# A fused convolution and state-space kernel on one core: the layer norm spread over three tiles, with a PSUM bank of its own

## What is computed

```
layer 0: two 3x3 convolutions with binary weights, batch norms, out = relu(y*scale + shift + x)
layer 1: mu, var over the 64 channels of each pixel
         xn = (x - mu) / sqrt(var + eps) * ln_g + ln_b
         the channels are cut into 4 chunks of 16; each is a sequence of 3136 steps
         y = chunk + mamba(chunk):
             xi, z = in_proj(chunk);  u = silu(conv4(xi));  dt, B, C = x_proj(u)
             delta = softplus(dt_proj(dt));  h = h*exp(delta*A) + delta*u*B;  y = h.C + u*D
             out_proj(y * silu(z))
layer 2: 1x1, grouped 3x3, 1x1 convolution, residual
layer 3: four directional scans with relu(conv)
```

## Time and profile before

| what | value |
|---|---|
| median of 3 runs | 9415.61 us (9406.84 to 9419.84) |
| the profiled execution's own time | 9422.56 us |
| its span, first to last instruction | 9419.6 us |
| mean granted clock of TensorE | 0.869 of full speed |
| busy in the span | PE 82%, DVE 70%, ACT 57%, POOL 54% |
| layer 1's loop, 16 pairs of 14 tiles | about 725 to 7070 us |

### The profile page before, as it was taken

The page is one execution under the profiler, slowest core; times in us unless marked ns, Lnnn a source line. Parts: engine busy times, 40 slices in busy tenths (PEclk is TensorE's granted clock), DMA queues, the critical chain, the costliest instruction groups (busy, mean ns, idle before and its releaser), DMA issues.

```text
span 9419.6 us, 132034 instructions
## 1 busy us (share of the span) xinstructions
PE 7733.7 (82%) x30601; PEld 4129.2 (44%) x30601; DVE 6595.7 (70%) x9126; ACT 5400.0 (57%) x9444; POOL 5115.0 (54%) x3388
## 2 busy tenths in 40 slices
PE   9977777777777777777787777777778999999996
PEld 9962222222222222222222222222224899959996
DVE  7748898898988989889898998989882122211222
ACT  0237777777777777777777777777770133201332
POOL 0007788887877878788787887878770000000000
PEclk9988788888878888788888888888888999999998
DMA  9646565665656556565565665655551000030002
GB/s 177 167 115 172 154 171 158 168 165 156 171 158 166 163 157 168 156 167 161 163 168 156 167 164 160 170 158 168 160 164 58 18 0 0 18 86 0 0 0 55
DMA packets 1108311, 1201.77 MB, mean 128 GB/s; under 512 B 460432, under 2 KB 1094800, under 8 KB 1107344
## 3 DMA queue, kind: packets, MB, share of 16 engines
q1 hardware_dynamic: 871568, 1117.24, 43.7%
q10 hardware_dynamic: 236032, 77.08, 3.5%
HBM read 961.04 MB, written 155.41 MB: 119 GB/s over the span
## 4 chain that ended last, share of the span: by engine, by line
PE 38%; issue 22%; DVE 16%; POOL 9%; ACT 8%; DVEq 1%; ACTq 1%; DMA 0%; POOLq 0%; SPq 0%
PE ps L921 18%; DVE ps L631 11%; PE ps L908 5%; DVE da L647 5%; POOL prod L658 4%; PE ps L226 3%; PE ps L417 3%; PE ps L669 3%; ACT da L621 2%; POOL dlt L551 2%; PE ps L431 2%; ACT L1020 1%; ACT L1018 1%; POOL lnx L503 1%; PE ps L666 1%
## 5 line engine op out<-in xcount | busy, mean ns | idle before, releaser
L658 POOL TENSOR_TENSOR prod<-da,bsp 128x896 f32<-128x896 f32 x1792 | 3439.5, 1927 | 1040.9 <-PE ps L669 702.7
L647 DVE TENSOR_TENSOR_SCAN da<-da,ps 128x449 f32<-128x449 f32 (+1 forms) x3584 | 3863.2, 1078 | 0.0
L631 DVE TENSOR_TENSOR ps<-ps,bsp 128x448 f32<-128x448 f32 x3585 | 2198.4, 613 | 767.7 <-PE ps L615 741.6
L621 ACT ACTIVATE da<-da,nega 128x448 f32<-128x448 f32 x3588 | 2257.6, 662 | 56.6 <-issue 48.1
L615 PE MATMUL ps<-stack,seld 96*128 96x448 bf16 x3587 | 1440.2, 416 | 810.3 <-DVE da L647 765.0
L921 PE MATMUL ps<-pv,ws 128*128 128x224 f32 x8800 | 1695.2, 355 | 9.4 <-ACT pv L1083 7.1
L921 PEld LDWEIGHTS ps<-pv,ws 128*128 128x128 f32 x8800 | 1660.2, 189 | 45.0 <-issue 7.7
L669 PE MATMUL ps<-prod,wc 128*32 128x448 f32 x7200 | 1405.8, 686 | 191.7 <-POOL prod L658 191.1
L615 PEld LDWEIGHTS ps<-stack,seld 96*128 96x128 bf16 x3587 | 356.1, 101 | 2335.9 <-DVE da L647 2016.8
L1247 DVE SCALAR_TENSOR_TENSOR pv<-ps,R 128x224 f32<-128x224 f32 x880 | 422.3, 480 | 1282.1 <-PE ps L921 1282.1
L417 PE MATMUL ps<-xn,wtap 128*128 128x448 f32 x1808 | 1017.3, 671 | 3.5 <-ACT bsp L477 3.5
(11 more groups left out here) (119 smaller groups left out, 7227.7 us busy)
## 6 DMA issues: line engine op xcount, KB each, us to landing
da<-delta_copy SPq DMA_DIRECT2D x3595, 224.0 KB, 3.5
stack<-parts SPq DMA_DIRECT2D x2700, 28.0 KB, 2.3
delta_copy<-dlt SPq DMA_DIRECT2D x225, 224.0 KB, 2.9
lnx<-in_x SPq DMA_DIRECT2D x118, 224.0 KB, 3.0
lny<-y_nchw SPq DMA_DIRECT2D x118, 224.0 KB, 4.1
x_column_pairs<-otile SPq DMA_DIRECT2D x225, 116.0 KB, 3.3
xpad<-x_column_pairs SPq DMA_DIRECT2D x32, 812.0 KB, 4.4
xpad<-in_x SPq DMA_DIRECT2D x64, 392.0 KB, 6.6
```

What stands on the lines that cost most here:

```text
L621: a.activation(elements(j, st.t), elements(j, st.t), ACT.Exp, scale=nega[:, j:j + 1])\
L631: v.tensor_tensor(du, du, bsp[:, st.t % 2, 0, :], ALU.mult).then_inc(S["dbu_done"], 1)
L647: v.tensor_tensor_scan(a, a, d, start, ALU.mult, ALU.add).then_inc(S["scan_done"], 1)
L658: g.tensor_tensor(prod[:, j % 8:j % 8 + 2, :], da[:, j:j + 2, lo:lo + T], bsp[:, st.t % 2, 1:2, :].to_broadcast([P, 2, T]), ALU.mult).then ...
```

## The change

The layer norm of a block no longer runs inside one tile. Its first part (`ln_in`: the loads, `scale_y`, `add_x`) runs in tiles 6 to 12, its middle (`ln_mid`: `relu`, `lnc`, `lnv`) one tile later, in tiles 7 to 13, its end (`ln_last`: `times_rstd`, `shift`) one tile later again, in tiles 8 to 13 and tile 0 of the next pair. The loads move from ahead of SP's slot 0 to slot 6. The number of instructions of each kind in the loop stays as it was.

The two matmuls write to bank 4, which only they use, and have semaphores of their own: `lnc` waits until ACT has read the previous `lnv` and for its input, `lnv` waits for ACT's square. They leave the list of tasks that take turns in banks 5 and 6, so all 14 tiles have the five tasks `u`, `z`, `bc0`, `dt`, `bc1` there. Ahead of the loop seven blocks are begun instead of six; the seventh does not do its end there.

```
-PE_AT = {0: ["tap0"], 1: ["last3", "tap1"], 2: ["tap2", "tap3"], 3: ["z"], 4: ["project"], 5: ["lnc"], 6: ["bc0"],
-         7: ["dt"], 8: ["sum0", "bc1"], 9: ["lnv"], 11: ["sum1"], 14: ["sum2"]}
-ACT_AT = {0: ["scale_y"], 2: ["cast0"], 3: ["relu"], 4: ["cast1"], 5: ["silu", "u", "z", "exp"], 6: ["evacuate"],
-          7: ["lnc"], 8: ["bc0"], 9: ["dt"], 10: ["dt2", "bc1"], 11: ["lnv"], 13: ["clamp"], 15: ["shift"]}
+PE_AT = {0: ["tap0"], 1: ["last3", "tap1"], 2: ["tap2", "tap3"], 3: ["z"], 4: ["project"], 6: ["bc0"], 7: ["dt"],
+         8: ["sum0", "bc1"], 10: ["lnc"], 11: ["sum1"], 13: ["lnv"], 14: ["sum2"]}
+ACT_AT = {2: ["cast0"], 3: ["relu"], 4: ["cast1"], 5: ["silu", "u", "z", "exp"], 6: ["evacuate"], 7: ["shift"],
+          8: ["bc0"], 9: ["dt"], 10: ["dt2", "bc1"], 11: ["scale_y"], 12: ["lnc"], 13: ["clamp"], 15: ["lnv"]}
-POOL_AT = {1: ["rest0", "add_x"], 5: ["rest1"], 9: ["over"], 11: ["delta"], 13: ["delta_u", "times_rstd"]}
-SP_AT = {1: ["copy"], 5: ["part0"], 7: ["part1"], 9: ["part2"], 12: ["store"]}
+POOL_AT = {1: ["rest0"], 3: ["times_rstd"], 5: ["rest1"], 9: ["over"], 11: ["delta"], 13: ["delta_u"], 15: ["add_x"]}
+SP_AT = {1: ["copy"], 5: ["part0"], 6: ["ln_load"], 7: ["part1"], 9: ["part2"], 12: ["store"]}
...
-        DU_BANK, TMP_BANK, Y_BANK, O_BANK = 0, 5, 7, 7
+        DU_BANK, LN_BANK, TMP_BANK, Y_BANK, O_BANK = 0, 4, 5, 7, 7
...
+                self.ln_in = Norm(p, t, 6) if 6 <= t <= 12 else None
+                self.ln_mid = Norm(p, t, 7) if t < 0 or 7 <= t <= 13 else None
+                self.ln_last = Norm(p, t, 8) if t == 0 or t >= 8 else None
...
+        def ln_centre(pe, st):
+            n = st.ln_mid.ln
+            if not (st.ahead and st.k == 0):
+                pe.wait_ge(S["var_copied"], n)
+            pe.wait_ge(S["x_relu"], n + 1)
+            pe.matmul(ps[:, LN_BANK, 0:T], wcs("centre", 0, P), xres[:, :], start=True, stop=True)\
+                .then_inc(S["centre_mm"], 1)
+
+        def ln_average(pe, st):
+            n = st.ln_mid.ln
+            pe.wait_ge(S["squared"], n + 1)
+            pe.matmul(ps[:, LN_BANK, 0:T], wcs("average", 0, P), xsq[:, :], start=True, stop=True)\
+                .then_inc(S["average_mm"], 1)
...
-            for k in range(6):
+            for k in range(7):
                 st = Ahead(k)
-                pe_task(pe, st, "lnc")
-                pe_task(pe, st, "lnv")
+                ln_centre(pe, st)
+                ln_average(pe, st)
```

More of the change, by code:

```diff
@@ L316, in build @@
         BC = ["bc0", "bc1"]
-        AHEAD = [(n, k) for k in range(6) for n in ("lnc", "lnv")] + [(n, 0) for n in ["u", "z", "dt"] + BC] + \
-            [(n, 1) for n in ("u", "z", "dt")]
+        AHEAD = [(n, 0) for n in ["u", "z", "dt"] + BC] + [(n, 1) for n in ("u", "z", "dt")]
         BASE = len(AHEAD)
@@ L323, in build @@
             for name in TASKS:
[L324 to L325 removed]
+                AT[(t, name)] = len(AT)
         ORDER = list(AT)
@@ L341, in drives, with __init__ @@
             return ps[:, DU_BANK + bank, lo:hi]
+        class Norm:
+            def __init__(self, p, t, first):
+                self.ahead = False
+                self.k = t - first if t >= first else t - first + ST
+                self.ln = p * KT + (self.k + (KT if t >= first else 0))
+                self.pair = (p + 1) % PAIRS
+                self.out = p * ST + t
+        class First:
+            def __init__(self, k):
+                self.ahead, self.k, self.ln, self.pair, self.out = True, k, k, 0, 0
         class Step:
@@ L370, in two_back @@
                 st = Step(self.p, t if i >= 0 else t - ST)
-                return back, st.next if back.startswith("bc") else st.ln if back.startswith("ln") else st.far
+                return back, st.next if back.startswith("bc") else st.far
         class Ahead:
@@ L478, in act_task @@
             elif name == "lnc":
-                if not (st.ahead and st.k == 0):
-                    a.wait_ge(S["xn_ready"], st.ln)
+                ln = st.ln_mid
+                if not (ln.ahead and ln.k == 0):
+                    a.wait_ge(S["xn_ready"], ln.ln)
                 a.copy(xcen[:, :], src).then_inc(S["centred"], 1)
@@ L483, in act_task, with ln_load @@
             else:
+                ln = st.ln_mid
                 a.activation(xvar[:, :], src, ACT.Ln, bias=vec_c(5)).then_inc(S["var_copied"], 1)
-                a.wait_ge(S["var_copied"], st.ln + 1)
+                a.wait_ge(S["var_copied"], ln.ln + 1)
                 a.activation(xrstd[:, :], xvar[:, :], ACT.Exp, scale=-0.5).then_inc(S["rstd"], 1)
[L489 to L492, removed]
+        def ln_load(sp, ln):
+            if not (ln.ahead and ln.k == 0):
+                sp.wait_ge(S["x_relu"], ln.ln)
+            a = ln.k * T
@@ L503, in ln_sum, with ln_relu, ln_scale @@
             g.tensor_tensor(lnx[:, :], lnx[:, :], lny[:, :], ALU.add).then_inc(S["x_summed"], 1)
[L505 to L508, removed]
+        def ln_relu(a, ln):
+            a.wait_ge(S["x_summed"], ln.ln + 1)
+            if not (ln.ahead and ln.k == 0):
+                a.wait_ge(S["centred"], ln.ln)
             a.activation(xres[:, :], lnx[:, :], ACT.Relu).then_inc(S["x_relu"], 1)
-        def ln_scale(g, st):
-            g.wait_ge(S["rstd"], st.ln + 1)
+        def ln_scale(g, ln):
+            g.wait_ge(S["rstd"], ln.ln + 1)
@@ L513, in ln_scale, with ln_shift @@
             g.tensor_tensor(xcen[:, :], xcen[:, :], xrstd[:, :], ALU.mult).then_inc(S["scaled"], 1)
[L515 to L519, removed]
+        def ln_shift(a, ln):
+            a.wait_ge(S["scaled"], ln.ln + 1)
+            if not ln.ahead:
+                a.wait_ge(S["out_mm"], ln.out + 2)
+            k = ln.k * T + 3
             a.activation(xn[:, k:k + T], xcen[:, :], ACT.Identity, bias=vec_c(1), scale=vec_c(0)).then_inc(S["xn_ready"], 1)
@@ L868, in _ @@
                                 conv_tap(pe, st, int(name[3:]))
-                            elif st.has_ln or not name.startswith("ln"):
+                            elif name == "lnc":
+                                if st.ln_mid:
+                                    ln_centre(pe, st)
+                            elif name == "lnv":
+                                if st.ln_mid:
+                                    ln_average(pe, st)
+                            else:
                                 pe_task(pe, st, name)
@@ L985, in _ @@
             a.wait_ge(S["ready"], 4)
[L986 to L992, removed]
+            for k in range(7):
+                ln = First(k)
+                ln_affine(a, ln)
+                ln_relu(a, ln)
+                act_task(a, Ahead(k), "lnc")
+                act_task(a, Ahead(k), "lnv")
+                if k < 6:
+                    ln_shift(a, ln)
             for k in range(2):
@@ L1264, in _ @@
             g.wait_ge(S["ready"], 4)
[L1265 to L1268, removed]
+            for k in range(7):
+                ln = First(k)
+                ln_sum(g, ln)
+                if k < 6:
+                    ln_scale(g, ln)
             st = Ahead(0)
@@ L1292, in _ @@
                                 rest_of(g, st, int(name[4]))
[L1293 to L1297, removed]
+                            elif name == "add_x":
+                                if st.ln_in:
+                                    ln_sum(g, st.ln_in)
+                            elif st.ln_last:
+                                ln_scale(g, st.ln_last)
             barrier(g, 3)
```

59 lines of the change are left out of this document (24 added, 35 removed).

## The result

The changed kernel takes 9091.33 us (median of 4 runs, 9089.95 to 9092.64), the kernel before beside it 9412.89 us (4 runs). The ratio is 0.9658, 95% interval 0.9641 to 0.9675. Forecast were 9105 us, in a range of 8960 to 9290. The profiled execution took 9091.03 us.

What follows compares the result with a forecast made beforehand. A ring through ACT and POOL, as long as the quiet tile, was taken to bound it beside DVE. Terms summed to 376.4 us a pair, 20.1 less; 16 x 20.1 - 10.6 = 311 us off gave 9112, so 9105, range 8960 to 9290.

Steps and rivals of the forecast that it cites:

- Waits removed: Bank waits of `lnc` and `dt`, `shift`'s and `relu`'s waits go; each tile starts at 25.34 us, 354.8 a pair.
- `add_x` in POOL's leg: At POOL's slot 15, between `over` and `rest0`, tiles 6 to 12: paid in full, 7.8 us a pair.
- `shift` in ACT's leg: At ACT's slot 7, tiles 8 to 13 and 0: costs 4.6 us a pair.
- `scale_y` and `lnc` ahead of `clamp`: On ACT, slots 11 and 12: POOL's `delta` waits for `clamp`, 1.04 us in tiles 7 to 12; sum 6.8.
- Free pieces: `relu` and `lnv` on ACT ahead of `cast1`, `times_rstd` on POOL between `rest0` and `over`: covered by idle time, no cost.
- The jump back: At the loop's top, ACT's jump before `cast0`: free by 1 us or up to 3.45; 1.0 a pair taken.
- PE's wait ahead of `lnv`: At PE's slot 13, waiting 2.2 us for ACT's squares; cost put at zero, between 0 and 3.8.
- Waits not shown by the rows: Other waits in ACT's leg of layer-norm tiles: 0.2 us a tile, 1.4 a pair, bounds 0 and 10.4.
- Ahead of the loop: One more block in series before the loop, hidden by nothing: 10.6 us.
- The rival in which DVE alone holds the tiles: DVE's work sets the tile time and the layer norm becomes free: 8759 us, or 8884 with `add_x` paid; 11%.
- The rival of a loss by `lnv`'s wait: PE's lead gives no cover, DVE stands 3.8 us in each of seven tiles: 9530 us; 5%.
- No change: The stalls only move and each tile with layer norm costs what it did; 4%.

Runs made afterwards that it cites:

- the spare POOL instruction at slot 3: The changed kernel with one more POOL addition of 128x448 on scratch tiles at slot 3 of tiles 1 to 5: 9090.07 us.
- The kernel with `lnv` later: The changed kernel with PE's `lnv` moved from slot 13 to slot 14, behind `sum2`: 9101.19 us.
- the spare instruction at slot 15: The changed kernel with one more POOL addition of 128x448 on scratch tiles at slot 15 of tiles 1 to 5: 9156.24 us.
- the last experiment: Against the one with both legs clear, ACT's instruction adding one to `dexp` left out of every tile, so the softplus is incomplete: 8664.71 us.
- the one with both legs clear: The changed kernel with `scale_y`, `lnc`, `shift` behind `clamp`, `lnv` at PE's slot 14, `add_x` at POOL's slot 3, loads a tile earlier: 8788.04 us.

## Why the prediction was right, step by step

The mechanism was right, and so were nearly all terms of the sum: a pair was put at 376.4 us and takes 375.3. That is 17 us of the 21 by which the profiled execution lies below the 9112 forecast for it.

1. *Waits removed.* The bank waits and `shift`'s wait went, and the quiet tiles stayed at 25.25 us. That `relu`'s wait on `add_x` would go was wrong. I took POOL's slot 15 of one tile to be earlier than ACT's slot 3 of the next, by the numbers of the slots. ACT runs ahead of POOL, and waits 1.76 us. It cost nothing, since it is spent ahead of `cast1`, where ACT waits for `rest0` in any case. In all, this wait is 198.4 us where it was 220.7.
2. *`add_x` in POOL's leg*: 7.8 us a pair put down. Taken out it gave 116 us (8904.45 to 8788.04), 7.3 a pair.
3. *`shift` in ACT's leg*: 4.6 put down; ACT's leg has 0.65 more, and taking it out gave 66 us, 4.1 a pair.
4. *`scale_y` and `lnc` ahead of `clamp`*: 6.8 put down. POOL waited 1.06 to 1.22 us a tile instead of 1.04, 123.1 us in all, 7.7 a pair; moving them behind `clamp` gave 121 us, 7.5 a pair. This is the term that was put too low. The slack of 0.48 us was read in one tile, and the wait is 1.06 us in one tile and 1.22 in the next.
5. *Free pieces*: the spare POOL instruction at slot 3 shows that this place costs nothing, and so did `times_rstd` and `add_x` together there. `relu` and `lnv` on ACT were free as well: in the tile shown ACT still waits 1.89 us for `rest0` behind them.
6. *The jump back*: 1.0 us a pair put down. ACT still stands at the loop's top, now 2.59 us, but POOL comes to `rest0` without a gap in the timeline of tile 0. Before, it had waited there 50.4 us in 15 pairs, for `cast0`; the trace after has no such wait, so none of it was paid:

```profile
2614.44 1.79 ACT L640 ACTIVATE da<-da,nega 128x448 f32<-128x448 f32 x3 [2.59 <-issue]
...
2615.11 3.66 POOL L677 TENSOR_TENSOR prod<-da,bsp 128x896 f32<-128x896 f32 x2
...
2618.73 1.03 POOL L587 TENSOR_TENSOR rest<-dlt,parts 128x448 f32<-128x448 f32 x1
```

7. *PE's wait ahead of `lnv`*: 2.2 us predicted, 2.52 measured. I had DVE covered by PE's lead; it is not quite, DVE waits 0.69 us behind it in the tile shown. That is free for another reason than the one I gave: DVE has 170.00 - 151.67 = 18.3 us of waits in these six tiles whatever their places. The kernel with `lnv` later has the wait removed and gains nothing.
8. *Waits not shown by the rows*: 1.4 put down, nothing found in the tile shown: `over` starts at 2868.67, 0.07 us after `dq` ends. Over a pair, the terms as the trace after has them are 354.8 + 7 x 1.13 for `add_x` + 7 x 0.65 for `shift` + 7.7 for `clamp` = 375.0, against 375.3 measured. That leaves 0.3 for this item and the jump together, of 2.4 put down. The 2.1 too much stood against the 0.9 that item 4 was too low, and that the sum came out within 1.1 is in part luck.
9. *Ahead of the loop*: 10.6 put down, 10.7 measured.

The rival in which DVE alone holds the tiles fell for this change, by the spare instruction at slot 15 and by the ring's waits in every tile. Only in the last experiment is DVE full too, at 99.3%. The Trainium skill (Perfetto Trace Analysis, "Identifying the Most-Contended Engine") names the engine with the highest occupancy as the one to optimise first. In this loop that was DVE, at 5624.92 of 6344.42 us. Yet the 619 us from the kernel before to the one with both legs clear (9407.02 to 8788.04) came with DVE's instructions as they were, busy 5624.92 and 5576.52 us. So the rule named the floor and not what held the tiles above it; the trace bears out the same page's section "Identifying Dependency Chains" rather, which has the reader follow the semaphores that are waited on. The rival of a loss by `lnv`'s wait fell: the wait came as described, at a place where it is not paid. No change and remaining waits fell by the tiles' times.

In two expectations, too, a size was off. The spare POOL instruction was put at 1.13 us and 90 us in all; it was 0.935 us long and cost 65. And I gave DVE's floor in a quiet tile as 24.85 us and so at most 0.4 us a tile to win by a shorter leg; the loop came to 5582.43 / 224 = 24.92 us a tile from 25.50, 0.58 less. The tiles' mean had been above the 25.34 of the six tiles read, and DVE's own busy time fell a little too, from 24.90 to 24.75 us a tile.

## What to carry to other kernels

Where two engines hand work back and forth once a tile, find the ring: the stretch on each engine from the instruction that waits for the other to the one that the other waits for. If both joints wait in every tile, the tile is as long as the two legs, and a piece of side work costs about all of its length inside a leg, and nothing outside as long as it fits into the wait at the joint, however idle its engine is. Before a bank or a buffer is added to end a wait, ask whether the waiting piece could stand elsewhere: here the bank alone gave 54 us, other slots alone gave 314, and four more pieces moved (`scale_y`, `lnc`, `shift`, `add_x`) gave 303 besides. Slot numbers of different engines can't be compared; read from a timeline which engine comes to its slot first.

## What was not expected of the hardware

POOL's addition of a 128x448 tile to itself took 0.935 us, that of two different tiles 1.14 us (L522 in the timeline after); the tile added to itself held zeros, and what makes the difference was not tested. TensorE's mean granted clock in the loop was 0.88 of full speed after and 0.83 before, and its busy time was 263 us less for the same matmuls. No part of the gain could be traced to that: neither leg of the tile shown waits for PE, and the clock does not go with the time from kernel to kernel. With the two matmuls back in banks 5 and 6 the profiled execution had a mean of 0.913 and took 9094.46 us; the changed kernel had 0.903 and took 9091.03.
